# New orders for five instruction queues in a cross-attention and feed-forward kernel, with four accumulating transfers moved among them

## The chip, the core and the metric

The kernel runs on one core of a Trainium2 chip. The core has five engines with a queue of instructions each: PE (TensorE, matrix products), DVE (VectorE), ACT (ScalarE), POOL (GpSimd) and SP (SyncE, which here only issues transfers). Every queue runs strictly in the order in which the program wrote it; semaphores tie the queues together. Sixteen DMA engines carry the transfers. The metric is the device time of one execution in microseconds.

## What is computed

The input is x and a context of 4 batches, 512 rows, 256 columns, in float32. Two blocks follow each other.

```python
# attention by autocorrelation: the softmax weights of the best 6 delays
qf, kf = rfft(q, axis=1), rfft(k, axis=1)
corr = irfft(qf * conj(kf)).mean(axis=-1)          # one row of 512 delays per head
weights, delays = top_k(corr, 6)                   # softmax of the weights
out = sum(w * v rolled by each delay) @ Wo.T + bo
x = x + out
# feed-forward with 8-bit activations and weights of -1, 0, 1
def bitlinear(x, w, b):
    xq = act_quant(rmsnorm(x)); wq = weight_quant(w)
    return einsum('bsd,fd->bsf', xq, wq) + b
x = x + bitlinear(gelu(bitlinear(layernorm(x), w1, b1)), w2, b2)
```

## The kernel before

Fourier transforms are matrix products with constant matrices. The first 77 us transform, project and correlate the four batches; the change does not touch that part. From there on two things run beside each other.

The late attention of batch n (0 to 3): `inverse(n, c)` on PE brings the product back from the frequencies, ACT copies half of it (`inverse_copy`), DVE combines (`inverse_out`), PE projects (`project`), DVE adds to the residual and takes row sums (`add_residual`). Then ACT centres the rows (`centre`, L665) and squares them (`square_x`, L673), DVE takes the row maxima (`row_max`, L975) and scales (`x_scales`, L979, L983), ACT rounds to integers (`round_x`, L681), DVE casts them to bf16 (`whole_x`, L998) and SP issues a DMA transpose of them (L311). POOL computes the scale that the bias of the first layer needs, from values of DVE (`x_deq`, L988, L992; `x_rms`, L1296 to L1302; `aug_parts`, L1309 to L1315), and SP transposes that as well (L313, the `aug` rows). Both transposes of batch n must have landed before the first of its four tiles can enter the feed-forward.

The feed-forward runs in 16 tiles t of 128 rows, four per batch. One tile passes through: `up(t)` on PE (L492, L494, hidden layer of 1024), `gelu(t)` on ACT (L691), `hidden_max(t)` (L1041), `h_inverse(t)` (L1046), `quantise_h(t)` (L1053) and `whole_h(t)` (L1059) on DVE, `turn_h(t)` on PE (L506, a transpose), `copy_h(t)` on ACT (L706), `down(t)` on PE (L516), and `finish(t)` on DVE (L1067), which scales, adds to the residual `res` and releases the store on SP (L316). Aside, ACT squares the hidden rows (`square(t)`, L700) and POOL makes the scale of the result out of them (`h_rms(t)`, L1277, L1279; `h_deq(t)`, L1288, L1290).

The last bias b2 is added to `res` by a transfer that accumulates, 512 KB for each batch, issued by POOL:

```python
def add_b2(n):
    pool.wait_ge(s["xc_made"], n + 1)
    pool.dma_start(res[:, n], b2_all[:].unsqueeze(1).broadcast_to([P, NA, D]), accum_op=ALU.add).then_inc(s[f"b2_added{n}"], 16)
```

`finish(4n)`, the first of its batch, waits until it has landed. Buffers are double (psum banks of `up`, `hq`, `hq_t`, `xc`) or fourfold (`wf`, one hidden tile each), and each reuse waits for its last reader: `down(t)` waits for `finish(t-2)`, `up(t)` for `gelu(t-2)`, `gelu(t)` for `quantise_h(t-4)` and `square(t-4)`, `hidden_max(t)` for `h_deq(t-4)`.

Nothing schedules at run time: the order of each queue is a list of such calls, written out by hand in the kernel, one list for each of PE, ACT, DVE and POOL, and two loops for SP. These lists are what the change rewrites. The names in them are those above.

Of the kernel before, what the change touches and what calls it, by code (L numbers as in the profile page):

```python
# [98 lines left out]
def build(nc, x, ctx, wq_t, wkv_t, wo_t, bq, bkv, bo, w1_t, b1, w2_t, b2, c_forward, c_signal, c_eye, c_parts, out):  # L99
    es = ExitStack()  # L100
    with es:
# [175 lines left out]
        def _(sp):  # L277
# [31 lines left out]
            for n in range(NB):  # L309
                sp.wait_ge(s["xq_made"], n + 1)  # L310
                sp.dma_start_transpose(xq_t[:, n].rearrange("p a c r -> p (a c) r"), xq[:].rearrange("p a d -> p (a d)")).then_inc(s[f"xq_in{n}"], 16)  # L311
                sp.wait_ge(s["aug_made"], n + 1)
                sp.dma_start_transpose(aug_t[:, n], aug.rearrange("p a k -> p (a k)")).then_inc(s[f"aug_in{n}"], 16)  # L313
            for t in range(NA * NB):
                sp.wait_ge(s["y_made"], t + 1)
                sp.dma_start(out_v[:, t // NA, t % NA], res[:, t // NA, t % NA]).then_inc(s["stored"], 16)  # L316
            sp.wait_ge(s["stored"], 16 * NA * NB)

        LATE = 4 * 16
# [3 lines left out]
        def _(pe):  # L323
# [239 lines left out]
            turn_h(7)  # L563
            turn_h(8)
            down(6)
            up(11)
            turn_h(9)
            down(7)
            up(12)
            down(8)  # L570
            turn_h(10)
            up(13)
            down(9)
            turn_h(11)
            up(14)
            down(10)
            turn_h(12)
            up(15)
            down(11)
            turn_h(13)  # L580
            down(12)
            turn_h(14)
            down(13)
            turn_h(15)
            down(14)
            down(15)
# [3 lines left out]
        def _(act):  # L590
# [118 lines left out]
            inverse_copy(0, 1)  # L709
            copy_corr_even(1)  # L710
            exponents(1)
            act.activation(warm[:], half_neg[:, 0:1], ACT.Gelu)
# [5 lines left out]
            round_x(0)  # L718
            centre(1)
            inverse_copy(2, 0)  # L720
            gelu(0)
            square_x(1)
            gelu(1)
            inverse_copy(2, 1)
            gelu(2)
            square(0)
            round_x(1)
            gelu(3)
            square(1)
            square(2)  # L730
# [15 lines left out]
            gelu(7)  # L746
            copy_h(3)
            copy_h(4)
            square(6)
            square(7)  # L750
            gelu(8)
            square(8)
            copy_h(5)
            square_x(3)
            copy_h(6)
            gelu(9)
            round_x(3)
            square(9)
            gelu(10)
            copy_h(7)  # L760
            copy_h(8)
            square(10)
            gelu(11)
            copy_h(9)
            square(11)
            gelu(12)
            copy_h(10)
            square(12)
            gelu(13)
            copy_h(11)  # L770
            square(13)
            gelu(14)
            copy_h(12)
            square(14)
            gelu(15)
            copy_h(13)
            square(15)
            copy_h(14)
            copy_h(15)

# [2 lines left out]
        def _(dve):  # L783
# [315 lines left out]
            whole_x(1)  # L1099
            x_deq(1)  # L1100
            h_inverse(1)
            add_residual(2, 1)
            hidden_max(3)
            quantise_h(1)
            whole_h(1)
            inverse_out(3, 0)
            h_inverse(2)
            row_max(2)
            inverse_out(3, 1)
            x_scales(2)  # L1110
            quantise_h(2)
            hidden_max(4)
            whole_h(2)
            x_deq(2)
            h_inverse(3)
            add_residual(3, 0)
            h_inverse(4)
            hidden_max(5)
            add_residual(3, 1)
            h_inverse(5)  # L1120
            quantise_h(3)
            whole_x(2)
            quantise_h(4)
            whole_h(3)
            whole_h(4)
            quantise_h(5)
            finish(0)
            finish(1)
            row_max(3)
            finish(2)  # L1130
            whole_h(5)
            hidden_max(6)
            finish(3)
            h_inverse(6)
            hidden_max(7)
            quantise_h(6)
            h_inverse(7)
            finish(4)
            hidden_max(8)
            whole_h(6)  # L1140
            h_inverse(8)
            quantise_h(7)
            whole_h(7)
            x_scales(3)
            quantise_h(8)
            whole_h(8)
            x_deq(3)
            hidden_max(9)
            whole_x(3)
            finish(5)  # L1150
            h_inverse(9)
            quantise_h(9)
            whole_h(9)
            hidden_max(10)
            finish(6)
            h_inverse(10)
            quantise_h(10)
            whole_h(10)
            finish(7)
            hidden_max(11)  # L1160
            finish(8)
            h_inverse(11)
            quantise_h(11)
            whole_h(11)
            hidden_max(12)
            finish(9)
            h_inverse(12)
            quantise_h(12)
            whole_h(12)
            hidden_max(13)  # L1170
            finish(10)
            h_inverse(13)
            quantise_h(13)
            whole_h(13)
            hidden_max(14)
            finish(11)
            h_inverse(14)
            quantise_h(14)
            whole_h(14)
            hidden_max(15)  # L1180
            finish(12)
            h_inverse(15)
# [8 lines left out]
        def _(pool):  # L1191
# [139 lines left out]
            pool.wait_ge(s["out_half_made"], 2 * NC)  # L1331
            out_spectrum(3)
            x_rms(1)
            aug_parts(1)
            h_rms(0)
            h_deq(0)
            h_rms(1)
            add_b2(0)
            h_deq(1)
            x_rms(2)  # L1340
            aug_parts(2)
            h_rms(2)
            h_rms(3)
            h_rms(4)
            add_b2(1)
            add_b2(2)
            h_deq(2)
            h_deq(3)
            h_rms(5)
            h_deq(4)  # L1350
            h_rms(6)
            h_rms(7)
            h_deq(5)
            add_b2(3)
            h_deq(6)
            h_deq(7)
            x_rms(3)
            aug_parts(3)
            h_rms(8)
            h_deq(8)  # L1360
            h_rms(9)
            h_deq(9)
            h_rms(10)
            h_deq(10)
            h_rms(11)
            h_deq(11)
            h_rms(12)
            h_deq(12)
            h_rms(13)
            h_deq(13)  # L1370
# [41 lines left out]
```

## Time and profile before

| | us |
|---|---|
| median of 3 runs (lowest, highest) | 171.93 (171.16, 172.03) |
| the profiled execution | 171.91 |
| its span, first to last instruction | 170.1 |
| busy PE, DVE, ACT, POOL in the span | 151.2, 129.9, 98.7, 87.6 |

The profiled execution is 1.8 us longer than its span, and lies at the median. The busy times are sums over the whole span. What limits a stretch is read from the waits in it: which engine stands still, and what it waits for when it goes on. "issue" as the releaser of a wait means that the profile shows no instruction of an engine that ended then; often it is a transfer that landed. The start of the first instruction is 0 us in all views.

### The profile page before, as it was taken

The page shows a single profiled execution, that of the slowest core. Times are in us where ns is not written, and L with a number is a line of the kernel's source. Part 1 is how long each engine was busy: PE and PEld are TensorE (multiplying, and loading weights), DVE is VectorE, ACT ScalarE, POOL GpSimd, SP SyncE. Part 2 cuts the span into 40 slices and gives each one's busy share as a digit, 9 for nine tenths or more (in the row PEclk, how much of TensorE's full clock was granted, in tenths as well). Part 3 has the DMA queues.
Part 4 walks back from the last instruction along what each step waited for, and adds up shares of the span by engine and source line. Part 5 has one row for each costly group of instructions (what it writes and reads, how often), then busy time and mean ns, then how long its engine had stood idle before and what let it go on. Part 6 is the DMA issues. An engine that isn't in the chain of part 4 may idle for free.

```text
span 170.1 us, 2666 instructions
## 1 busy us (share of the span) xinstructions
PE 151.2 (89%) x808; PEld 103.9 (61%) x814; DVE 129.9 (76%) x325; ACT 98.7 (58%) x198; POOL 87.6 (51%) x156
## 2 busy tenths in 40 slices
PE   7889899999899999998999999799994499699853
PEld 2534689558654785756678854676763267457542
DVE  1546479999759996268578999999999139999982
ACT  3127624819570443120189189979998097999911
POOL 2040697945931000593943239678794706766330
PEclk9999999999999999999999999999999579999999
DMA  5989999162088000000000310046269760472012
GB/s 174 343 274 348 363 360 265 31 89 34 0 123 123 2 4 0 0 2 0 0 6 0 72 21 0 4 93 95 29 104 154 123 90 0 92 245 69 31 62 93
DMA packets 20529, 16.65 MB, mean 98 GB/s; under 512 B 7586, under 2 KB 19747, under 8 KB 20516
## 3 DMA queue, kind: packets, MB, share of 16 engines
q1 hardware_dynamic: 16292, 12.30, 24.1%
q0 software_dynamic: 4224, 4.19, 17.4%
q8 instruction: 6, 0.10, 0.2%
q14 instruction: 7, 0.06, 0.1%
HBM read 8.61 MB, written 2.10 MB: 63 GB/s over the span
## 4 chain that ended last, share of the span: by engine, by line
PE 45%; DVE 20%; ACT 11%; issue 11%; POOL 7%; DMA 4%; SPq 1%; DVEq 0%; POOLq 0%; ACTq 0%
PE psum L390 12%; PE psum L403 5%; DVE hmax L1041 4%; PE psum L474 4%; DMA res<-in_x 4%; PE psum L461 3%; PE psum L516 3%; DVE c_f L1053 3%; PE psum L332 3%; PE psum L333 3%; PE psum L492 2%; ACT kv_f L608 2%; PE psum L416 2%; ACT xn L673 2%; ACT xc_and_least L665 2%
## 5 line engine op out<-in xcount | busy, mean ns | idle before, releaser
L390 PE MATMUL psum<-wkv,c_f 128*128 128x512 f32 x64 | 29.0, 598 | 0.8 <-ACT c_f L595 0.8
L691 ACT ACTIVATE wf<-psum,xdeq 128x1024 f32<-128x1024 f32 x16 | 17.9, 1121 | 5.6 <-PE psum L494 5.6
L492 PE MATMUL psum<-w1q,xq_t 128*128 128x512 bf16 x58 | 15.8, 392 | 5.3 <-issue 5.2
L390 PEld LDWEIGHTS psum<-wkv,c_f 128*128 128x128 f32 x64 | 11.8, 190 | 13.7 <-issue 12.4
L614 ACT COPY kv_f<-psum 128x512 f32<-128x512 f32 x16 | 9.2, 582 | 18.1 <-PE psum L390 18.1
L1041 DVE TENSOR_REDUCE hmax<-wf 128x1 f32<-128x1025 f32 x16 | 19.3, 1212 | 0.1
L516 PE MATMUL psum<-w2q,kv_f 128*128 128x256 bf16 x128 | 17.1, 279 | 0.3 <-ACT kv_f L706 0.3
L461 PE MATMUL psum<-to_signal,out_f 128*128 128x256 f32 x64 | 15.1, 384 | 0.9 <-issue 0.8
L474 PE MATMUL psum<-wo,out_t 128*128 128x256 f32 x64 | 14.8, 385 | 1.2 <-DVE out_t L956 1.2
L403 PE MATMUL psum<-wq,x_f 128*128 128x256 f32 x64 | 15.1, 381 | 0.8 <-ACT x_f L595 0.8
L1220 POOL TENSOR_TENSOR kv_f<-kv_f,bkv_dc 1x512 f32<-1x512 f32 x4 | 5.7, 1417 | 19.0 <-ACT kv_f L614 19.0
L403 PEld LDWEIGHTS psum<-wq,x_f 128*128 128x128 f32 x64 | 12.0, 190 | 4.8 <-issue 3.5
L516 PEld LDWEIGHTS psum<-w2q,kv_f 128*128 128x128 bf16 x128 | 12.4, 101 | 3.6 <-ACT kv_f L706 0.4
L1067 DVE SCALAR_TENSOR_TENSOR res<-psum,hdeq,res 128x256 f32<-128x256 f32 x16 | 7.6, 476 | 8.4 <-issue 6.7
L474 PEld LDWEIGHTS psum<-wo,out_t 128*128 128x128 f32 x64 | 11.8, 190 | 3.5 <-DVE out_t L956 1.7
L461 PEld LDWEIGHTS psum<-to_signal,out_f 128*128 128x128 f32 x64 | 11.8, 190 | 3.4 <-issue 1.7
L506 PE MATMUL psum<-eye,kv_f 128*128 128x128 bf16 x128 | 9.9, 225 | 4.4 <-DVE kv_f L1059 3.1
L506 PEld LDWEIGHTS psum<-eye,kv_f 128*128 128x128 bf16 x128 | 8.4, 101 | 7.0 <-DVE kv_f L1059 5.6
L492 PEld LDWEIGHTS psum<-w1q,xq_t 128*128 128x128 bf16 x64 | 5.9, 99 | 10.9 <-issue 6.2
L1053 DVE TENSOR_SCALAR c_f<-wf,hinv 128x1024 int16<-128x1024 f32 x16 | 12.3, 766 | 0.3
L595 ACT COPY c_f<-psum 128x512 f32<-128x512 f32 x8 | 4.6, 586 | 12.9 <-PE psum L333 12.9
L706 ACT COPY kv_f<-psum 128x512 int32<-128x512 int32 x16 | 9.3, 594 | 4.4 <-PE psum L506 4.4
(167 smaller groups left out, 353.1 us busy)
## 6 DMA issues: line engine op xcount, KB each, us to landing
ctx_in<-in_ctx SPq DMA_DIRECT2D x4, 512.0 KB, 5.6
res<-in_x SPq DMA_DIRECT2D x4, 512.0 KB, 6.9
res<-bo_all POOLq DMA_DIRECT2D x4, 512.0 KB, 5.2
res<-b_all POOLq DMA_DIRECT2D x4, 512.0 KB, 7.1
out<-res SPq DMA_DIRECT2D x16, 128.0 KB, 1.8
wf<-in_w_t SPq DMA_DIRECT2D x1, 1024.0 KB, 9.5
wf<-in_w_t SPq DMA_DIRECT2D x2, 512.0 KB, 10.6
wkv<-in_wkv_t SPq DMA_DIRECT2D x1, 512.0 KB, 7.3
```

The lines of the kernel that those rows point to most:

```text
L390: mm = pe.matmul(bank(K_BANKS + ft), c_f[:, c, ft * P:(ft + 1) * P], wkv[:, c, :], start=(c == 0), stop=(c == NC - 1))
L403: mm = pe.matmul(psum[:, Q_BANKS + fam, part * D:(part + 1) * D], x_f[:, c, ft * P:(ft + 1) * P], wq[:, c, :], start=(c == 0), stop=(c == ...
L461: mm = pe.matmul(psum[:, I_BANKS + c, fam * D:(fam + 1) * D], out_f[:, n % 2, fam, part, c * P:(c + 1) * P], to_signal[:, ft, :], start=(f ...
L474: mm = pe.matmul(psum[:, O_BANKS + half, k * D:(k + 1) * D], out_t[:, c, SLOT[a], :], wo[:, c, :], start=(c == 0), stop=(c == NC - 1))
L492: pe.matmul(dst, xq_t[:, m, j, c, :], w1q[:, c, cols], start=(c == 0), stop=False)
L506: mm = pe.transpose(t_bank(t % 2)[:, k * P:(k + 1) * P], hq[:, t % 2, k * P:(k + 1) * P], eye16[:])
L516: mm = pe.matmul(psum[:, Y_BANKS + t % 2, 0:D], hq_t[:, t % 2, k, :], w2q[:, k, :], start=(k == 0), stop=(k == NK - 1))
L614: act.copy(kv_f[:, n, ft, :], bank(K_BANKS + ft)).then_inc(s["kv_copied"], 1)
L691: act.activation(hid[j], hb, ACT.Gelu, scale=xdeq[:, m, j:j + 1]).then_inc(s["hid_made"], 1)
L706: act.copy(hq_t[:, t % 2].rearrange("p k r -> p (k r)").bitcast(I32), t_bank(t % 2).bitcast(I32)).then_inc(s["ht_copied"], 1)
L1041: dve.tensor_reduce(hmax[:, j:j + 1], hid_and_least[j], AX.X, ALU.max, apply_absolute_value=True).then_inc(s["hmax_made"], 1)
L1053: dve.tensor_scalar(hround[:, t % 2, :], hid[j], hinv[:, j:j + 1], 127.0, ALU.mult, ALU.mult).then_inc(s["hround"], 1)
```

## The change

The lists of PE, ACT, DVE and POOL from the late attention on hold the same calls as before, each exactly once, in another order. SP's two loops become three functions and a written list. No instruction is added or removed, and none changes its size or its waits. The four calls of `add_b2` come later in POOL's list. The call that makes ACT load the table for Gelu moves from ahead of `centre(0)` to behind `round_x(0)`. The diff, cut to the parts that the prediction speaks of:

```diff
+            def bring_x(n):
                 sp.wait_ge(s["xq_made"], n + 1)
...
+            def store(t):
                 sp.wait_ge(s["y_made"], t + 1)
...
+            bring_x(2)
+            bring_aug(2)
+            store(0)
+            store(1)
+            store(2)
+            bring_x(3)
+            bring_aug(3)
+            store(3)
...
 PE
             up(4)
-            up(5)
             turn_h(0)
             project(3, 0)
             project(3, 1)
+            up(5)
             turn_h(1)
+            down(0)
             turn_h(2)
             up(6)
-            down(0)
             up(7)
             down(1)
-            down(2)
             turn_h(3)
             turn_h(4)
+            down(2)
             down(3)
             up(8)
             turn_h(5)
-            down(4)
             up(9)
             up(10)
             turn_h(6)
+            down(4)
             down(5)
...
 ACT
             square_x(2)
             gelu(4)
             square(3)
+            round_x(2)
+            copy_h(0)
             square(4)
             gelu(5)
-            copy_h(0)
-            round_x(2)
+            copy_h(1)
             centre(3)
-            copy_h(1)
             gelu(6)
+            square(5)
             copy_h(2)
-            square(5)
             gelu(7)
             copy_h(3)
+            square(6)
+            square_x(3)
             copy_h(4)
-            square(6)
+            gelu(8)
+            round_x(3)
+            gelu(9)
...
 DVE
             inverse_out(2, 0)
+            hidden_max(1)
             h_inverse(0)
+            inverse_out(2, 1)
+            h_inverse(1)
+            hidden_max(2)
             quantise_h(0)
-            whole_h(0)
-            inverse_out(2, 1)
-            hidden_max(1)
-            hidden_max(2)
             add_residual(2, 0)
             whole_x(1)
...
+            x_deq(3)
+            whole_h(7)
+            whole_x(3)
+            hidden_max(8)
             finish(4)
-            hidden_max(8)
-            whole_h(6)
             h_inverse(8)
...
+            finish(11)
-            h_inverse(14)
...
             quantise_h(15)
             whole_h(15)
+            finish(12)
             finish(13)
             finish(14)
             finish(15)
```

How the instructions now stand is seen best at two places. The first is POOL around the transfer of b2 for batches 1 and 2 (`res<-b_all`, where `x2` means two of them behind each other). Before it stood right behind the three `h_rms` of tiles 2 to 4, ahead of `h_deq(2)`:

```order
L1277 TENSOR_TENSOR hms<-hss,eps 128x1
L1279 TENSOR_TENSOR hr<-hms,half_neg 128x1
L1320 DMA res<-b_all 128x4x256 x2
L1288 TENSOR_TENSOR hm<-hmax,hr 128x1
L1290 TENSOR_TENSOR hdeq<-hm,wdeq 128x1
L1288 TENSOR_TENSOR hm<-hmax,hr 128x1
L1290 TENSOR_TENSOR hdeq<-hm,wdeq 128x1
L1277 TENSOR_TENSOR hms<-hss,eps 128x1
L1279 TENSOR_TENSOR hr<-hms,half_neg 128x1
```

Now the one for batch 1 stands alone behind `h_rms(5)`, ahead of `x_rms(3)` (lines have moved by 29 in the changed kernel):

```order
L1317 TENSOR_TENSOR hm<-hmax,hr 128x1
L1319 TENSOR_TENSOR hdeq<-hm,wdeq 128x1
L1317 TENSOR_TENSOR hm<-hmax,hr 128x1
L1319 TENSOR_TENSOR hdeq<-hm,wdeq 128x1
L1306 TENSOR_TENSOR hms<-hss,eps 128x1
L1308 TENSOR_TENSOR hr<-hms,half_neg 128x1
L1349 DMA res<-b_all 128x4x256
L1325 TENSOR_TENSOR xv<-xss,eps 128x4
L1327 TENSOR_TENSOR xve<-xv,eps 128x4
L1331 TENSOR_TENSOR xr<-xve,half_neg 128x4
```

The transfers of b2 thus moved behind later tiles: batch 1 behind `h_rms(5)`, batch 2 behind `h_deq(7)`, batch 3 behind `h_rms(12)`, where before they stood behind `h_rms(4)`, `h_rms(4)` and `h_deq(5)`.

The second place is ACT behind `square_x(2)`, where `xround` is the rounding of batch 2, `wf` a Gelu, `prod` and `x_f` the squares and `kv_f` a copy of a turned tile. Before:

```order
L673 ACTIVATE xn,xss<-xc_and_least 128x256 x4
L691 ACTIVATE wf<-psum,xdeq 128x1024
L700 ACTIVATE prod,hss<-wf 128x1024
L700 ACTIVATE x_f,hss<-wf 128x1024
L691 ACTIVATE wf<-psum,xdeq 128x1024
L706 COPY kv_f<-psum 128x512
L681 ACTIVATE xround<-xc_and_least,xscale 128x256 x4
L665 ACTIVATE xc_and_least<-res,row_sum 128x256 x4
```

And now:

```order
L702 ACTIVATE xn,xss<-xc_and_least 128x256 x4
L720 ACTIVATE wf<-psum,xdeq 128x1024
L729 ACTIVATE prod,hss<-wf 128x1024
L710 ACTIVATE xround<-xc_and_least,xscale 128x256 x4
L735 COPY kv_f<-psum 128x512
L729 ACTIVATE x_f,hss<-wf 128x1024
L720 ACTIVATE wf<-psum,xdeq 128x1024
L735 COPY kv_f<-psum 128x512
L694 ACTIVATE xc_and_least<-res,row_sum 128x256 x4
```

The rounding of batch 2 moved ahead of `square(4)`, `gelu(5)` and `copy_h(0)`.

## Rows read from the trace of the kernel before

**Rows 1.** The page's busy times and its clock row (40 slices of the span)

```profile
PE 151.2 (89%) x808; PEld 103.9 (61%) x814; DVE 129.9 (76%) x325; ACT 98.7 (58%) x198; POOL 87.6 (51%) x156
...
PEclk9999999999999999999999999999999579999999
```

**Rows 2.** Waits from 95 us on: us in total, times, longest

```profile
DVE res L1067 <- issue: 6.7, 2, 6.4
```

**Rows 3.** Timeline of DVE: start, duration, shape; in brackets the idle time before

```profile
105.15 1.38 DVE L1059 CAST kv_f<-c_f 128x1024 bf16<-128x1024 int16 x1
...
138.81 0.48 DVE L1067 SCALAR_TENSOR_TENSOR res<-psum,hdeq,res 128x256 f32<-128x256 f32 x1 [6.35 <-issue]
...
157.55 0.47 DVE L1067 SCALAR_TENSOR_TENSOR res<-psum,hdeq,res 128x256 f32<-128x256 f32 x1
...
160.39 0.47 DVE L1067 SCALAR_TENSOR_TENSOR res<-psum,hdeq,res 128x256 f32<-128x256 f32 x1
...
166.61 0.48 DVE L1067 SCALAR_TENSOR_TENSOR res<-psum,hdeq,res 128x256 f32<-128x256 f32 x1 [1.20 <-PE psum L516]
167.49 0.48 DVE L1067 SCALAR_TENSOR_TENSOR res<-psum,hdeq,res 128x256 f32<-128x256 f32 x1 [0.39 <-PE psum L516]
```

**Rows 4.** Timeline of PE around `up(8)` (the row at 134.04)

```profile
123.43 1.04 PE L516 MATMUL psum<-w2q,kv_f 128*128 128x256 bf16 x8
124.30 1.03 PE L492 MATMUL psum<-w1q,xq_t 128*128 128x512 bf16 x4
...
128.86 1.05 PE L516 MATMUL psum<-w2q,kv_f 128*128 128x256 bf16 x8 [0.26 <-ACT kv_f L706]
134.04 1.49 PE L492 MATMUL psum<-w1q,xq_t 128*128 128x512 bf16 x3 [4.12 <-issue]
```

**Rows 5.** Timeline of SP's two transposes of batch 2

```profile
123.67 1.23 SPq L311 DMA_TRANSPOSE xq_t<-xq  x1
124.95 2.58 SPq L313 DMA_TRANSPOSE aug_t<-c_sum  x1
```

**Rows 6.** Transfers issued between 108 and 121 us: KB, us to landing

```profile
res<-b_all POOLq DMA_DIRECT2D x1, 512.0 KB, 5.5
xq_t<-xq SPq DMA_TRANSPOSE x1, 3.0
aug_t<-c_sum SPq DMA_TRANSPOSE x1, 2.5
```

**Rows 7.** The same between 121 and 132 us

```profile
res<-b_all POOLq DMA_DIRECT2D x2, 512.0 KB, 9.2
xq_t<-xq SPq DMA_TRANSPOSE x1, 5.8
aug_t<-c_sum SPq DMA_TRANSPOSE x1, 8.6
```

**Rows 8.** POOL's line L1320 (`add_b2`), all four: its landings

```profile
DMA to landing us min/median/max: 5.5/7.1/10.4
```

**Rows 9.** Timeline of POOL: b2 for batches 1 and 2, and for batch 3

```profile
123.06 3.30 POOL L1320 DMA_DIRECT2D res<-b_all  x2
...
133.24 1.31 POOL L1320 DMA_DIRECT2D res<-b_all  x1
```

**Rows 10.** Timeline of ACT: table for Gelu, `centre(1)`, `square`, `gelu`, `copy_h`, `round_x`

```profile
86.00 1.28 ACT L712 ACT_TABLE_LOAD   x1
...
98.32 1.71 ACT L665 ACTIVATE xc_and_least<-res,row_sum 128x256 f32<-128x256 f32 x4 [4.24 <-DVE row_sum L966]
...
118.50 1.06 ACT L700 ACTIVATE x_f<-wf 128x1024 f32<-128x1024 f32 x1
...
119.54 1.11 ACT L691 ACTIVATE wf<-psum,xdeq 128x1024 f32<-128x1024 f32 x1
120.54 0.58 ACT L706 COPY kv_f<-psum 128x512 int32<-128x512 int32 x1
121.00 1.72 ACT L681 ACTIVATE xround<-xc_and_least,xscale 128x256 int16<-128x256 f32 x4
```

More of the change, by code:

```diff
@@ L711, in _ @@
             exponents(1)
-            act.activation(warm[:], half_neg[:, 0:1], ACT.Gelu)
             centre(0)
@@ L718, in _ @@
             round_x(0)
+            act.activation(warm[:], half_neg[:, 0:1], ACT.Gelu)
             centre(1)
@@ L721, in _ @@
             gelu(0)
+            gelu(1)
             square_x(1)
-            gelu(1)
             inverse_copy(2, 1)
             gelu(2)
+            round_x(1)
             square(0)
-            round_x(1)
             gelu(3)
@@ L736, in _ @@
             square(3)
+            round_x(2)
+            copy_h(0)
             square(4)
             gelu(5)
-            copy_h(0)
-            round_x(2)
+            copy_h(1)
             centre(3)
-            copy_h(1)
             gelu(6)
+            square(5)
             copy_h(2)
-            square(5)
             gelu(7)
             copy_h(3)
+            square(6)
+            square_x(3)
             copy_h(4)
-            square(6)
+            gelu(8)
+            round_x(3)
+            gelu(9)
+            copy_h(5)
+            gelu(10)
+            copy_h(6)
             square(7)
-            gelu(8)
             square(8)
[L753 to L757, printed above, removed]
+            copy_h(7)
             square(9)
-            gelu(10)
-            copy_h(7)
+            gelu(11)
+            square(10)
+            gelu(12)
             copy_h(8)
-            square(10)
-            gelu(11)
+            square(11)
+            gelu(13)
             copy_h(9)
-            square(11)
-            gelu(12)
+            square(12)
             copy_h(10)
-            square(12)
-            gelu(13)
-            copy_h(11)
             square(13)
             gelu(14)
+            gelu(15)
+            square(14)
+            copy_h(11)
+            square(15)
             copy_h(12)
-            square(14)
-            gelu(15)
             copy_h(13)
-            square(15)
             copy_h(14)
@@ L1091, in _ @@
             inverse_out(2, 0)
+            hidden_max(1)
             h_inverse(0)
+            inverse_out(2, 1)
+            h_inverse(1)
+            hidden_max(2)
             quantise_h(0)
-            whole_h(0)
-            inverse_out(2, 1)
-            hidden_max(1)
-            hidden_max(2)
             add_residual(2, 0)
             whole_x(1)
+            quantise_h(1)
             x_deq(1)
-            h_inverse(1)
+            hidden_max(3)
             add_residual(2, 1)
-            hidden_max(3)
@@ L1104, in _ @@
-            quantise_h(1)
+            whole_h(0)
+            h_inverse(2)
             whole_h(1)
+            quantise_h(2)
+            h_inverse(3)
             inverse_out(3, 0)
-            h_inverse(2)
+            inverse_out(3, 1)
             row_max(2)
-            inverse_out(3, 1)
+            quantise_h(3)
             x_scales(2)
-            quantise_h(2)
             hidden_max(4)
             whole_h(2)
-            x_deq(2)
-            h_inverse(3)
             add_residual(3, 0)
@@ L1117, in _ @@
             h_inverse(4)
+            add_residual(3, 1)
+            quantise_h(4)
+            x_deq(2)
+            whole_x(2)
+            whole_h(3)
             hidden_max(5)
-            add_residual(3, 1)
+            finish(0)
             h_inverse(5)
[L1121 to L1124, printed above, removed]
+            quantise_h(5)
             whole_h(4)
-            quantise_h(5)
-            finish(0)
+            hidden_max(6)
             finish(1)
@@ L1129, in _ @@
             row_max(3)
+            whole_h(5)
             finish(2)
-            whole_h(5)
-            hidden_max(6)
+            x_scales(3)
             finish(3)
             h_inverse(6)
+            quantise_h(6)
             hidden_max(7)
-            quantise_h(6)
+            whole_h(6)
             h_inverse(7)
+            quantise_h(7)
+            x_deq(3)
+            whole_h(7)
+            whole_x(3)
+            hidden_max(8)
             finish(4)
-            hidden_max(8)
@@ L1140, in _ @@
-            whole_h(6)
             h_inverse(8)
-            quantise_h(7)
-            whole_h(7)
-            x_scales(3)
             quantise_h(8)
-            whole_h(8)
-            x_deq(3)
             hidden_max(9)
-            whole_x(3)
             finish(5)
             h_inverse(9)
+            finish(6)
             quantise_h(9)
+            hidden_max(10)
+            whole_h(8)
             whole_h(9)
-            hidden_max(10)
-            finish(6)
+            finish(7)
             h_inverse(10)
+            hidden_max(11)
@@ L1157, in _ @@
             quantise_h(10)
[L1158 to L1161, printed above, removed]
+            hidden_max(12)
             h_inverse(11)
             quantise_h(11)
+            whole_h(10)
             whole_h(11)
-            hidden_max(12)
-            finish(9)
+            finish(8)
+            hidden_max(13)
             h_inverse(12)
             quantise_h(12)
+            h_inverse(13)
+            finish(9)
+            finish(10)
+            hidden_max(14)
@@ L1169, in _ @@
             whole_h(12)
-            hidden_max(13)
-            finish(10)
-            h_inverse(13)
             quantise_h(13)
+            h_inverse(14)
             whole_h(13)
-            hidden_max(14)
+            hidden_max(15)
+            quantise_h(14)
             finish(11)
-            h_inverse(14)
-            quantise_h(14)
+            h_inverse(15)
             whole_h(14)
-            hidden_max(15)
-            finish(12)
-            h_inverse(15)
             quantise_h(15)
@@ L1333, in _ @@
             x_rms(1)
+            h_rms(0)
             aug_parts(1)
-            h_rms(0)
+            h_rms(1)
             h_deq(0)
-            h_rms(1)
+            h_deq(1)
+            h_rms(2)
             add_b2(0)
-            h_deq(1)
             x_rms(2)
+            h_rms(3)
             aug_parts(2)
-            h_rms(2)
-            h_rms(3)
             h_rms(4)
-            add_b2(1)
-            add_b2(2)
             h_deq(2)
@@ L1363, in _ @@
             h_rms(10)
+            h_rms(11)
             h_deq(10)
-            h_rms(11)
+            h_rms(12)
+            add_b2(3)
             h_deq(11)
-            h_rms(12)
             h_deq(12)
```

46 lines of the change are left out of this document (31 added, 15 removed).

## The prediction

> **What bounds the kernel now.** I read the busy times first, then the waits of the late part, then the engines' timelines about the longest wait, and the transfers last. Over the whole span PE is busiest [rows 1], but the change begins behind 100 us, and there DVE sets the pace. Two numbers say so. A full round of DVE for one tile (`hidden_max`, `finish`, `h_inverse`, `quantise_h`, `whole_h`) takes 160.39 - 157.55 = 2.84 us, and DVE does such rounds back to back up to the tail [rows 3]; PE's share of a tile is `up` 1.30 us (six products of 512 columns, where eight of 256 take 124.30 - 123.43 = 0.87), `down` those 0.87, and `turn_h`, with half of `down`'s columns, 0.43, so 2.6 us [rows 4]. And from 102.39 us (`hidden_max(0)`) to 167.97 us (end of `finish(15)`) DVE stands still in four places only: 6.35 us ahead of `finish(4)`, 1.20 and 0.39 us ahead of the last two `finish` [rows 3], and 0.32 us more that make up the 6.7 us of two waits [rows 2].
>
> The 6.35 us have a history. `finish(4)` waits for `down(4)`, which stands behind `up(8)` on PE. `up(8)` stood ready from 129.9 us and began at 134.04, "issue" being its releaser [rows 4]: it waited for the transposes of batch 2. SP issued these at 123.67 and 124.95 us [rows 5]; they took 5.8 and 8.6 us to land [rows 7], the second so until 133.5 us, where those of batch 1 took 3.0 and 2.5 us [rows 6]. What lay beside them were two accumulating transfers of b2, issued from 123.06 us on [rows 9], with 9.2 us to landing as their median [rows 7] against 5.5 us for the one that went alone [rows 6]. While PE stood still its granted clock fell to 0.5, the level of 1.2 GHz [rows 1]: three matrix products of 0.5 us pitch instead of 0.22 [rows 4]. So `up(8)`, `turn_h(5)` and `down(4)`, 2.6 us of work, took from 134.04 until `finish(4)` could begin at 138.81.
>
> **The change, on paper.** No work is added or removed, so the new end follows from where engines will stand still. I laid out the four lists from 102.39 us on, each call at the later of its engine being free and its waits being met, with pitches (start to start) from rows: ACT `gelu` 1.00, `copy_h` 0.47, `square` 1.04, `centre`, `square_x` and `round_x` 1.6 each [rows 10]; PE as above; DVE 1.13 for a maximum, 0.78 for `quantise_h`, 0.34 for a cast, 0.39 for `finish` and 0.12 for `h_inverse`, together 2.8 [rows 3] (only the sum has a row here); POOL 1.3 for issuing b2 [rows 9] and, rounded, 0.8 for `h_rms` and 0.6 for `h_deq`, on which nothing below rests closely. The steps that decide:
>
> 1. *Start.* `whole_h(0)` took 1.38 us [rows 3] where a cast takes 0.4, and stood ahead of `inverse_out(2, 1)`. Now it stands behind. `inverse_out(2, 1)` ends at 106.1 instead of 107.2, PE projects 1.1 us earlier, `whole_x(1)` ends at 109.1, the aug rows of batch 1 are ready at 111.5, and with 2.5 us to land `up(4)` begins at 114.2 instead of 114.9.
> 2. *Transposes of batch 2.* ACT has `square_x(2)` done at 115.6, `gelu(4)`, `square(3)` at 117.7 and `round_x(2)` at 119.3. DVE reaches `x_deq(2)` and `whole_x(2)` at 121.1 to 121.8 (1.8 us earlier), POOL makes the aug rows until 122.6. SP issues at 121.8 and 123.1, and alone they land at 124.9 and 125.6.
> 3. *b2 of batch 1* now waits behind `h_rms(5)`, so for `square(5)`, done at 126.05: issue at 126.9, behind these transposes. That is the separation.
> 4. *`up(8)`* is then held by PE itself: `down(2)` and `down(3)`, the latter behind `copy_h(3)` at 128.0, end at 128.9. It begins at 128.9, 5.1 us earlier, and PE never stands still long enough to repeat the 4.1 us ahead of the clock's fall; the longest gap I find is 1.1 us.
> 5. *Batch 3 of x* is brought forward: `square_x(3)` until 130.6, `round_x(3)` until 133.7, `whole_x(3)` at 133.8 to 134.15, transposes at 134.2 and 135.5, landed by 138.1. `up(12)` wants them at 140.1 only. DVE waits 0.3 us for `round_x(3)`. SP has only three stores ahead, released by 128.5; `store(3)` and later ones queue for 7 us, and nobody waits for them but the end.
> 6. *`finish(4)`* begins at 135.3 instead of 138.81, with `hidden_max(8)`, `whole_h(6)`, `quantise_h(7)`, `whole_h(7)` and batch 3's scales, cast and x_deq (3.7 us of DVE work) already behind it.
> 7. *From there to the end* DVE has 22.5 us of work by the pitches (12 `finish`, 8 `h_inverse`, `quantise_h` and casts each, 7 maxima), and waits 0.4 us ahead of `hidden_max(14)` and 1.35 us in the tail, where `turn_h(15)`, `copy_h(15)` and `down(15)` follow `whole_h(15)` as before. ACT has 21.5 us left from 133.7 and PE 20 us from 134.8, both less than DVE. `finish(15)` ends near 159.9, before any stretching.
>
> The same as a sum over DVE: idle before 8.26 us and the stretched cast 1.04 make 9.3. New idle: 0.3 ahead of `whole_x(3)`, 0.4 ahead of `hidden_max(14)`, 0.4 in hand-overs, 1.35 in the tail, 2.45 in all. Gain 6.85 us. The 1.6 us by which DVE's other rows in this stretch exceeded their pitches I let recur. Span 170.1 - 6.85 = 163.25; with the 1.8 us outside it, 165.1 us. The profiled execution was at the median, so nothing is corrected.
>
> **Edits at nothing.** The table load of 1.28 us moves into a stretch in which ACT stood idle for 4.24 us [rows 10], and it held nobody where it was. If that cover were gone it would cost 1.3 us. The last store begins at the end of `finish(15)` as before.
>
> **Where the new waits can bite: b2.** The transfers had slack before and have little now. `finish(4)` at 135.3 needs a landing after issue at 126.9: 8.4 us of room. `finish(8)` at 146.4 needs one after issue at 139.2 (behind `square(7)`, `h_rms(7)` and `h_deq(7)`): 7.2 us. `finish(12)` at 156.8, issue 148.4: 8.4 us. What stands behind each on DVE is everything, and `down(6)`, `down(10)`, `down(14)` wait for them. Landings ran 5.5 to 10.4 us [rows 8]; alone 5.5, beside another b2 and transposes 8.0 and more. In the new order none has a transpose or a second b2 beside it, so I take 5.5 to 7, at no cost; at 10.4 each the three would cost 2.0, 3.2 and 2.0 us if they did not absorb each other, about 5 together since a late one delays the next deadline more than the next issue. Stores of 128 KB do lie beside the second and third.
>
> A row bears on POOL's side as well: two issues took 3.30 us, one 1.31 [rows 9], and the cast of 1.38 us lay beside a POOL operation [rows 3]. The Trainium skill, page "SBUF — State Buffer", section "🔬 SBUF: two separate sides", says that DVE in a two-port mode (casts and `tensor_scalar` among them) locks GpSimd out while it writes the descriptors of its own transfers, so that such a transfer starves. By that rule this change puts b2 of batches 2 and 3 into DVE's densest stretch and the landings go to the long end; the trace, where a stretched issue cost 0.3 us, bears it out weakly.
>
> **Rivals.**
> - *b2 lands late.* The landings take about 10 us because POOL's issue is stretched or stores share the DMA engines; DVE waits ahead of `finish(4)`, `(8)` and `(12)`. For it: 10.4 was seen. Against it: only with a second transfer and two transposes beside. Time 165.1 + 5 = 170 us. Chance 0.15.
> - *The transposes were slow by themselves.* If 5.8 and 8.6 us were not b2's doing but SP's (its second issue took 2.58 us [rows 5]), they land at 131.7, `up(8)` is 2.8 us late and `up(12)` 4.0 us, of which the first delay covers most: 165.1 + 4 = 169 us. Against it: batch 1 with 3.0 and 2.5 [rows 6]. Chance 0.06.
> - *Slower than before.* The place is `finish(8)`, whose queue is in order. If b2 of batch 2 lands L us after its issue, all behind it moves by L - 7.2. Slower begins at L = 7.2 + 6.8 = 14.0 us; with 15.5 the time is 173.4 us. It takes five stores and a starved issue together; the largest L seen is 10.4. Chance 0.05.
> - *The wait only moves.* ACT has no slack from 115.7 to 139 us in my layout; if each of its steps comes 5% late with PE behind, the 6.35 us come back as many small waits of DVE, and the time stays near 171.5. Against it: in the tail of before the same calls ran beside DVE's rounds of 2.84 us without a wait [rows 3]. Chance 0.04.
>
> **The numbers.** The forecast has 0.70, with its own range of 163.2 (no stretches recur) to 167.5 (b2 a little late, some hand-overs more). The whole range goes to 169.5, into the first two rivals, and down to 162.8. A measurement of this kernel tells about 0.5%, 0.9 us, from no change. Faster: 0.70, 0.13 of the first rival's 0.15, 0.06 of the second and a little of the last, 0.90. Same: 0.05. Slower: 0.05.
>
> **What will show it.** Right: no wait of DVE ahead of a `finish` above 1.5 us; `up(8)` begins near 129 with PE's clock at full level throughout; every transpose lands within 3.5 us and each b2 within 7.5; `finish(4)` near 135. Wrong: "issue" ahead of `finish(4)`, `(8)` or `(12)` (b2), ahead of `up(8)` or `up(12)` (transposes), or DVE's idle time spread over many small waits for ACT.

## The result and the profile after

The changed kernel takes 165.32 us (median of 4 runs, 164.24 to 165.50) against 171.55 us for the one before (median of 4, 170.93 to 172.03): a ratio of 0.963, with a 95% interval of 0.957 to 0.968. The forecast was 165.1 us. The profiled execution took 165.38 us with a span of 163.6. An execution more than 1.5% above the fastest of its kernel counts as slow and stays out of the ratios below: there is one of the kernel before (174.0 us) and one in experiment 8 (169.06 us).

The first rows to read are those that answer to [rows 1]. Every engine is busy for as long as before, within 2 us (the largest difference is DVE's, 129.9 against 128.2), in a span that is 6.5 us shorter, and PE's clock never fell:

```profile
PE 150.5 (92%) x814; PEld 102.9 (63%) x814; DVE 128.2 (78%) x325; ACT 98.9 (60%) x198; POOL 87.3 (53%) x156
...
PEclk9999999999999999999999999999999999999999
```

DVE's waits from 100 us on, in the changed kernel (us in total, times, longest), answer to [rows 2]. The wait of 6.4 us on "issue" is gone, and no wait on a transfer is left; nine short ones that are left sum to 3.8 us:

```profile
DVE res L1096 <- PE psum L545: 2.0, 4, 1.3
...
DVE hmax L1070 <- ACT wf L720: 0.7, 2, 0.5
DVE res L995 <- PE psum L503: 0.6, 2, 0.4
...
DVE kv_f L1088 <- PE psum L535: 0.5, 1, 0.5
```

The timeline of PE about `up(8)` (start, duration) answers to [rows 4]. `up(8)` is the row at 129.94, right behind `down(2)` and `down(3)`, and has no idle time before it:

```profile
127.66 0.61 PE L535 MATMUL psum<-eye,kv_f 128*128 128x128 bf16 x8 [0.21 <-ACT kv_f L735]
128.10 2.01 PE L545 MATMUL psum<-w2q,kv_f 128*128 128x256 bf16 x16
129.94 1.03 PE L521 MATMUL psum<-w1q,xq_t 128*128 128x512 bf16 x4
```

The transfers answer to [rows 5 to 9]. First SP's and POOL's timelines in the changed kernel: the second transpose of batch 2 is issued 3.9 us ahead of b2 of batch 1, and those of batch 3 lie between two transfers of b2:

```profile
122.75 1.23 SPq L312 DMA_TRANSPOSE xq_t<-xq  x1
124.02 1.27 SPq L316 DMA_TRANSPOSE aug_t<-c_sum  x1
...
135.19 1.23 SPq L312 DMA_TRANSPOSE xq_t<-xq  x1
```

```profile
127.88 1.44 POOL L1349 DMA_DIRECT2D res<-b_all  x1
...
140.53 1.34 POOL L1349 DMA_DIRECT2D res<-b_all  x1
```

And what was issued between 119.5 and 132 us, with the us to landing:

```profile
res<-b_all POOLq DMA_DIRECT2D x1, 512.0 KB, 7.1
...
xq_t<-xq SPq DMA_TRANSPOSE x1, 3.2
aug_t<-c_sum SPq DMA_TRANSPOSE x1, 2.5
```

The landings of all four b2, which answer to [rows 8]:

```profile
DMA to landing us min/median/max: 5.5/5.9/7.1
```

Last, three `finish` of DVE in the changed kernel, tiles 4, 14 and 15, which answer to [rows 3]. `finish(4)` comes without a wait at 136.21, and the tail has its 1.26 and 0.39 us as before:

```profile
136.21 0.47 DVE L1096 SCALAR_TENSOR_TENSOR res<-psum,hdeq,res 128x256 f32<-128x256 f32 x1
...
160.09 0.48 DVE L1096 SCALAR_TENSOR_TENSOR res<-psum,hdeq,res 128x256 f32<-128x256 f32 x1 [1.26 <-PE psum L545]
160.96 0.48 DVE L1096 SCALAR_TENSOR_TENSOR res<-psum,hdeq,res 128x256 f32<-128x256 f32 x1 [0.39 <-PE psum L545]
```

One offset has to be taken out before two traces are laid over each other. The part that the change does not touch ended at different times: the first transpose is issued at 94.94 us in the trace of before and at 95.81 in that of after, and over the thirteen traces of this study it lies near 94.6 to 95.0 or near 95.7 to 96.1, in both groups with old and with new orders. The offset is there long before the change begins: PE's third group of Fourier products starts at 24.27 us in the trace of before and at 25.15 in that of after. Below, "late part" is the span less the start of that first transpose: 75.2 us before, 67.8 us after, 7.4 us less. The times that were measured differ by 6.2 us. So a median of a few executions can be off by about 1 us for this reason alone, and steps below 1 us are read from the late part. That is one trace for each kernel, and before has a second spread: its executions have a mean granted clock of PE of 0.98, with spans from 169.9 us, or of 0.99, with spans from 169.0, and the profiled one is of the first kind. Its 75.2 us, and with it the first step of the ladder below, may be too large by up to about 1 us.

### The profile page after: what moved, and what is told of

Read it like the earlier page. It is cut to its first block and busy times, and to the rows that moved or that the text cites. A ratio compares the mean times of both kernels' runs of the same rounds, so it can differ in the third digit from the quotient of the medians.

```text
span 163.6 us, 2672 instructions
## 1 busy us (share of the span) xinstructions
PE 150.5 (92%) x814; PEld 102.9 (63%) x814; DVE 128.2 (78%) x325; ACT 98.9 (60%) x198; POOL 87.3 (53%) x156
## 5 line engine op out<-in xcount | busy, mean ns | idle before, releaser
L545 PE MATMUL psum<-w2q,kv_f 128*128 128x256 bf16 x128 | 16.2, 273 | 1.4 <-ACT kv_f L735 1.4
L521 PE MATMUL psum<-w1q,xq_t 128*128 128x512 bf16 x64 | 16.4, 379 | 0.9 <-issue 0.9
L490 PE MATMUL psum<-to_signal,out_f 128*128 128x256 f32 x64 | 15.1, 384 | 0.9 <-issue 0.8
L432 PE MATMUL psum<-wq,x_f 128*128 128x256 f32 x64 | 15.1, 381 | 0.8 <-ACT x_f L624 0.8
L1249 POOL TENSOR_TENSOR kv_f<-kv_f,bkv_dc 1x512 f32<-1x512 f32 x4 | 5.2, 1294 | 19.6 <-ACT kv_f L643 19.6
L545 PEld LDWEIGHTS psum<-w2q,kv_f 128*128 128x128 bf16 x128 | 11.7, 98 | 5.0 <-ACT kv_f L735 3.4
L535 PE MATMUL psum<-eye,kv_f 128*128 128x128 bf16 x128 | 9.4, 219 | 1.9 <-ACT kv_f L735 1.1
L1308 POOL TENSOR_TENSOR hr<-hms,half_neg 128x1 f32<-128x1 f32 x16 | 10.4, 648 | 1.3
```

The lines of the kernel that those rows point to most:

```text
L432: mm = pe.matmul(psum[:, Q_BANKS + fam, part * D:(part + 1) * D], x_f[:, c, ft * P:(ft + 1) * P], wq[:, c, :], start=(c == 0), stop=(c == ...
L490: mm = pe.matmul(psum[:, I_BANKS + c, fam * D:(fam + 1) * D], out_f[:, n % 2, fam, part, c * P:(c + 1) * P], to_signal[:, ft, :], start=(f ...
L521: pe.matmul(dst, xq_t[:, m, j, c, :], w1q[:, c, cols], start=(c == 0), stop=False)
L535: mm = pe.transpose(t_bank(t % 2)[:, k * P:(k + 1) * P], hq[:, t % 2, k * P:(k + 1) * P], eye16[:])
L545: mm = pe.matmul(psum[:, Y_BANKS + t % 2, 0:D], hq_t[:, t % 2, k, :], w2q[:, k, :], start=(k == 0), stop=(k == NK - 1))
L1308: pool.tensor_tensor(hr[:, p], hms[:, p], half_neg[:, 0:1], ALU.pow).then_inc(s["hr_made"], 1)
```

## The experiments

**1. b2 apart, nothing else.** The kernel before, with POOL's list changed in three places:

```diff
-            add_b2(1)
-            add_b2(2)
...
             h_rms(5)
+            add_b2(1)
...
-            add_b2(3)
...
             h_deq(7)
+            add_b2(2)
...
             h_rms(12)
+            add_b2(3)
```

> The kernel before with one edit: add_b2(1), (2), (3) stand on POOL behind h_rms(5), h_deq(7) and h_rms(12), as in the changed kernel; all other lists as before. Theory (b2 beside the transposes made the wait): the transposes of batch 2 land in 3.0 and 2.5 us, up(8) begins at 129.9 instead of 134.0 us, finish(4) at about 133.9 (held by b2 of batch 1, issued at 128.3), DVE's wait of 6.35 us shrinks to 1.4, PE's clock stays at full level; time 171.5 - 5 = 166.6 us, about 0.97 of before. Rival (the order of the other queues brings most of it): time 169 us or more.

Measured: 168.15 us, ratio 0.976 (0.969 to 0.984). The transfers issued between 119.5 and 132 us, with the us to landing, and after them DVE's waits for b2:

```profile
res<-b_all POOLq DMA_DIRECT2D x1, 512.0 KB, 6.6
xq_t<-xq SPq DMA_TRANSPOSE x1, 3.3
aug_t<-c_sum SPq DMA_TRANSPOSE x1, 2.6
```

```profile
DVE res L1067 <- DMA res<-b_all: 2.1, 1, 2.1
```

The transposes are fast again and the clock stays up, as the theory said; the late part is 71.0 us, 4.2 less than before. The gain was to be 5, and the time 166.6 us: b2 of batch 1 landed after 6.6 us, not 5.5, and DVE waited 2.1 us for it instead of 1.4, and the untouched part came out 0.85 us longer than in the trace of before. So separating alone brings more than half, and it makes a smaller wait of its own.

**2. The collision put back into the changed kernel.** On POOL:

```diff
             h_rms(3)
+            add_b2(1)
+            add_b2(2)
             aug_parts(2)
             h_rms(4)
             h_deq(2)
             h_deq(3)
             h_rms(5)
-            add_b2(1)
...
-            add_b2(2)
```

> The changed kernel with one edit: add_b2(1) and (2) stand together behind h_rms(3), so that they are in flight when the transposes of batch 2 are issued. Theory: issued at 119.6 to 121.2 us, they overlap the transposes issued near 122.8 and 124.0; these land after 4 to 6 and 6 to 9 us, up(8) begins 1.5 to 3 us late; time 167 to 168.5 us. Rival (only the orders of the other queues count, or the transposes are slow by themselves): 165.3 us.

Measured: 166.52 us, ratio to before 0.967 (0.962 to 0.973), late part 69.0 us, 1.2 more than the changed kernel. That is a little less than expected. From issue to landing the two transposes took 15.1 us in sum, against 14.4 in [rows 7], and PE waited for them (transfers issued between 119.5 and 132 us; then PE's row of `up(8)`):

```profile
res<-b_all POOLq DMA_DIRECT2D x2, 512.0 KB, 7.7
...
xq_t<-xq SPq DMA_TRANSPOSE x1, 8.2
aug_t<-c_sum SPq DMA_TRANSPOSE x1, 6.9
```

```profile
131.64 1.02 PE L521 MATMUL psum<-w1q,xq_t 128*128 128x512 bf16 x4 [1.65 <-DMA xq_t<-xq]
```

But b2 had been issued 3.0 us ahead of the first transpose (119.62 against 122.62; in before it was 0.6 us), so all had landed by 131.5 us. PE's wait was 1.65 us, and the clock did not fall. A wait of that length is no safeguard, though: in experiment 5 PE waits 1.63 us at the same call, and there the clock falls. The mechanism holds in both kernels; its price depends on how long after PE's readiness the last transpose lands (1.5 us here, 3.6 in before) and on whether the clock falls.

**3. No b2 at all in the kernel before** (b2 is left out of the output): `add_b2` issues nothing, `finish` does not wait.

> The kernel before without the four transfers of b2 and the waits for them (the bias b2 is left out of the output). Theory: the wait of 6.35 us ahead of finish(4) goes nearly whole, time 171.5 - 6 = 165.5 us, less than with b2 apart by what its landing still costs there (1.4 us). Rival (the transposes are slow by themselves): transposes of 5.8 and 8.6 us remain and the time stays near 171.

Measured: 166.17 us, ratio 0.968 (0.962 to 0.974), late part 69.7 us. The transposes of batch 2 took 3.2 and 2.5 us, so they are not slow by themselves. DVE's wait ahead of `finish(4)` is down to nothing, 0.9 us of new waiting appears for `x_rms(3)`, and the gain is 5.5 us of late part, not 6.

**4. No b2 in the changed kernel** (b2 is left out of the output).

> The changed kernel without the four transfers of b2 and the waits for them (the bias b2 is left out of the output). Theory (in the new order b2 costs nothing): 165.3 us, at most 0.4 less. Rival (b2 still holds finish or slows transfers): 164 us or less.

Measured: 164.78 us, ratio 0.958 (0.952 to 0.963), late part 67.75 us against 67.8. The time is 0.5 us less than that of the changed kernel, where the forecast allowed 0.4, but the single executions pair off (165.31, 165.15, 164.41 and 164.22 against 165.50, 165.38, 165.27 and 164.24), so no cost is to be seen. In the new order the four transfers cost nothing: 2 MB of accumulating traffic that cost the old order 5.5 us is hidden.

**5. Plain copies instead of accumulating ones.** In the kernel before, for batches 1 and 2 (b2 is left out of their output):

```diff
-                pool.dma_start(res[:, n], b2_all[:]..., accum_op=ALU.add)
+                pool.dma_start(kv_f[:, n]..., b2_all[:]...)
```

> The kernel before, where the transfers of b2 for batches 1 and 2 are plain copies of the same 512 KB each into a free tile instead of accumulating ones (b2 is left out of the output for those batches). Theory A (any traffic of POOL beside a transpose slows it): the transposes land after 5 to 6 and 8 to 9 us, the time is 171.5. Theory B (accumulating is what costs, since a DMA engine reads its target as well): the transposes land in 3 to 4 us each, time about 166.5.

Measured: 170.25 us, ratio 0.988 (0.981 to 0.995), late part 72.4 us, between the two theories. The transfers issued between 119.5 and 132 us, and PE's row of `up(8)`:

```profile
kv_f<-b_all POOLq DMA_DIRECT2D x2, 512.0 KB, 5.1
xq_t<-xq SPq DMA_TRANSPOSE x1, 6.4
aug_t<-c_sum SPq DMA_TRANSPOSE x1, 6.4
```

```profile
132.68 1.61 PE L492 MATMUL psum<-w1q,xq_t 128*128 128x512 bf16 x4 [1.63 <-issue]
```

Plain traffic delays a transpose too: 6.4 us against 3.2 and 2.5 alone. The accumulating pair took longer to land (9.2 us as its median against 5.1), and beside it the second transpose took 8.6 us; that this transpose is late because the pair lasts longer fits, but was not tested apart. DVE's wait ahead of `finish(4)` fell from 6.35 to 3.62 us. PE stood still for only 1.63 us, yet its clock fell as `up(8)` began: the four products took 1.61 us where they take 1.03 at full clock. So part of what is left against experiment 3 (72.4 against 69.7 us) is the clock.

**6. The start on DVE.** The kernel of experiment 1 and

```diff
-            whole_h(0)
             inverse_out(2, 1)
+            whole_h(0)
```

> The kernel before with b2 apart (as in the first experiment) and inverse_out(2, 1) ahead of whole_h(0) on DVE. Theory: whole_h(0) no longer takes 1.4 us where PE waits for inverse_out(2, 1), up(4) begins 0.7 us sooner, and the time is 0.5 to 0.8 us less than with b2 apart alone. Rival: later queues absorb it, no difference from b2 apart.

Measured: 166.36 us, ratio 0.968 (0.964 to 0.972), late part 70.1 us, 0.9 less than experiment 1, a little above the 0.5 to 0.8 of the theory. The medians differ by 1.8 us, but the untouched parts of the two traces differ by 1.2 (first transpose at 94.60 against 95.79 us).

**7. `finish(4)` later.** The kernel of experiment 6 and

```diff
-            finish(4)
             hidden_max(8)
             whole_h(6)
             h_inverse(8)
             quantise_h(7)
+            finish(4)
```

> The kernel of the experiment on the start (before, b2 apart, inverse_out(2, 1) ahead of whole_h(0)) with one more edit on DVE: finish(4) stands behind hidden_max(8), whole_h(6), h_inverse(8) and quantise_h(7). Theory (what is left against the changed kernel, 2.3 us, is the 2.0 us for which DVE stood still ahead of finish(4) until b2 of batch 1 had landed): 2.4 us of DVE work now lie over that wait, and the time falls by 1.5 to 2.0 us to 164.3 to 164.9. Rival (the earlier x steps of batch 3 and the other moves of PE and ACT bring it): at most 0.8 us less, 165.6 or more.

Measured: 165.27 us, ratio 0.9615 (0.957 to 0.966), late part 68.6 us, 1.5 less than experiment 6, and the wait for b2 is gone from DVE's waits. The work now lies over it. The median fell by 1.1 us only and misses the forecast of 164.3 to 164.9 by 0.4; four of the six executions took 165.02 to 165.47 and two 166.09 and 166.37. It is still below the rival's 165.6. With this the old lists, with five calls moved, are within 0.8 us of late part of the full rewrite.

**8. b2 of batch 2 later in the changed kernel**, behind `h_deq(9)`:

```diff
             h_deq(7)
-            add_b2(2)
...
             h_deq(9)
+            add_b2(2)
```

> The changed kernel with add_b2(2) two tiles later on POOL, behind h_deq(9) instead of h_deq(7). Theory (room of 7.1 us between issue and finish(8), of which a landing takes 5.5 to 7): issue near 143.3 us instead of 140.5, finish(8) 1.1 to 2.7 us late, time 166.4 to 168. Rival (the room is larger, or the loss is absorbed): 165.3.

Measured: 166.55 us (median of three executions, 165.82 to 167.25), ratio 0.969 (0.963 to 0.975), late part 70.8 us, 3.0 more than the changed kernel. POOL's issue and DVE's `finish(8)`:

```profile
143.36 1.34 POOL L1349 DMA_DIRECT2D res<-b_all  x1
```

```profile
148.87 0.48 DVE L1096 SCALAR_TENSOR_TENSOR res<-psum,hdeq,res 128x256 f32<-128x256 f32 x1 [2.37 <-DMA res<-b_all]
```

Counted from the first transpose it was issued 4.0 us later than in the changed kernel (143.36 - 94.61 against 140.53 - 95.81), and DVE waits 2.37 us, so 1.6 us had been in hand, as the room of 7.1 us less a landing of 5.5 says. The mechanism of the rival on the slow side is real, and its point is where the prediction put it. Not all of the 3.0 us is that wait: counted from the first transpose, `finish(8)` is 2.45 us late, and then PE's clock falls in the tail of this trace too (length, PE, PEld, DVE, ACT, POOL, then granted clock, DMA share, GB/s):

```profile
156.00:158.00 2.00, 2.00 (x11) 1.36 (x10) 1.36 (x5) 0.60 (x2) 1.12 (x2) 0.50 0.01 2
```

**9. SP's stores last in the changed kernel**, as the old loops had them:

```diff
-            store(0)
-            store(1)
-            store(2)
             bring_x(3)
             bring_aug(3)
+            store(0)
+            store(1)
+            store(2)
```

> The changed kernel with SP's list as before: store(0) to (2) behind the transposes of batch 3 instead of ahead. Theory: nobody waits for stores but the end, so 165.3 us within 0.4. Rival (stores beside the transposes of batch 3 or b2 of batch 2 slow them): b2 of batch 2 or the transposes land later by 1 us and more, 166 us.

Measured: 164.31 us, ratio 0.959 (0.952 to 0.965): no cost. The time is 1.0 us below the forecast of 165.3, as is the next experiment's: executions of the changed kernel itself lie near 164.2 or near 165.4. Three executions took 164.26 to 164.32 us; the profiled one took 166.12, and its trace shows where the time went: PE's clock fell in the tail, and its late part is 69.3 us, 1.5 more than that of the changed kernel. The 24 products of 256 columns that begin at 154.18 us took 4.45 us, where the same ones of the changed kernel took 2.91. Busy time of each engine in three stretches of it (length, PE, PEld, DVE, ACT, POOL, then granted clock, DMA share, GB/s):

```profile
150.00:152.00 2.00, 1.38 (x13) 0.72 (x11) 1.54 (x3) 1.62 (x3) 1.64 (x7) 1.00 0.74 144
152.00:154.00 2.00, 0.88 (x13) 0.74 (x14) 2.00 (x5) 2.00 (x5) 1.47 (x4) 1.00 1.19 198
154.00:156.00 2.00, 2.00 (x17) 1.50 (x14) 1.08 (x2) 1.12 (x3) 1.56 (x5) 0.57 0.33 57
```

And the same place of the changed kernel's own trace, 0.8 us later, with the same order on PE:

```profile
151.00:153.00 2.00, 1.16 (x12) 0.64 (x10) 1.59 (x3) 1.62 (x3) 1.56 (x7) 1.00 0.88 166
153.00:155.00 2.00, 1.10 (x17) 0.96 (x18) 2.00 (x4) 2.00 (x4) 1.38 (x5) 1.00 1.19 200
155.00:157.00 2.00, 2.00 (x21) 1.59 (x19) 1.85 (x6) 1.49 (x4) 1.80 (x4) 1.00 0.19 34
```

**10. The Gelu table back ahead of `centre(0)`** in the changed kernel.

> The changed kernel with the Gelu table loaded ahead of centre(0), as before. Theory: the load of 1.28 us lies in ACT's idle time in both places, 165.3 us within 0.3. Rival: the time at centre(0) matters, 0.4 us or more either way.

Measured: 164.28 us, ratio 0.959 (0.955 to 0.963), late part 67.8 us, the same to 0.1 us. The time is 1.0 us under the forecast of 165.3, which by itself would be the rival's sign; but the offset is there at 24.10 us against 25.15, long before the table is loaded at 85.73 us. And the first transpose, at 94.66 us, starts where it does in two traces with the table in its new place (94.61 and 94.71 in experiments 8 and 11). So no effect is seen.

**11. A better tail for the changed kernel**, on PE and on ACT:

```diff
             turn_h(12)
-            turn_h(13)
             down(11)
+            turn_h(13)
             down(12)
-            down(13)
             turn_h(14)
+            down(13)
             turn_h(15)
...
             gelu(15)
-            square(14)
             copy_h(11)
-            square(15)
+            square(14)
             copy_h(12)
+            square(15)
```

> The changed kernel with another tail: PE has down(11) ahead of turn_h(13) and turn_h(14) ahead of down(13), ACT has copy_h(11) and copy_h(12) one square earlier. Theory (PE and ACT, not DVE, lose 1.3 us behind whole_h(15) because turn_h(14) queues behind three downs): finish(15) starts 0.5 to 0.8 us earlier, time 164.6 to 164.8 us. Rival (the end is set by DVE's work up to whole_h(15)): 165.3 us.

Measured: 163.67 us (163.61 to 163.85, 6 runs), ratio 0.954 (0.951 to 0.958), so faster than before beyond doubt. Its interval overlaps slightly with that of the changed kernel (0.957 to 0.968). Experiment 10, timed beside it and as fast as the changed kernel by its late part, is the closer comparison: 164.28 us (164.11 to 165.37, 6 runs), above every run here. The late part is 67.3 us, 0.5 less than that of the changed kernel, as the theory said. The forecast of the time, 164.6 to 164.8, started from 165.3, and this trace is of the group whose untouched part is 1 us shorter. DVE's wait ahead of `finish(14)` fell from 1.26 to 0.84 us:

```profile
158.51 0.48 DVE L1096 SCALAR_TENSOR_TENSOR res<-psum,hdeq,res 128x256 f32<-128x256 f32 x1 [0.84 <-PE psum L545]
```

The late parts of the traces make a ladder, from one edit to the next (one trace each; the steps hold in this order of edits):

| | late part, us | step |
|---|---|---|
| before | 75.2 | |
| b2 apart | 71.0 | -4.2 |
| and `whole_h(0)` behind `inverse_out(2, 1)` | 70.1 | -0.9 |
| and `finish(4)` behind four calls of tiles 6 to 8 | 68.6 | -1.5 |
| all the new orders | 67.8 | -0.8 |
| and the better tail | 67.3 | -0.5 |

## Why the prediction was right

The number was right and so was nearly every step under it. Laid beside the trace of after, less the 0.88 us by which its `hidden_max(0)` came later (103.27 against 102.39):

| step of the prediction | forecast | trace less 0.88 |
|---|---|---|
| 1: `up(4)` begins | 114.2 | 114.2 |
| 2: transposes of batch 2 issued | 121.8, 123.1 | 121.9, 123.1 |
| 3: b2 of batch 1 issued | 126.9 | 127.0 |
| 4: `up(8)` begins | 128.9 | 129.1 |
| 5: `whole_x(3)` begins | 133.8 | 133.9 |
| 6: `finish(4)` begins | 135.3 | 135.3 |
| b2 of batch 2 issued; `finish(8)` | 139.2; 146.4 | 139.7; 146.7 |
| 7: `finish(15)` ends | 159.9 | 160.6 |

*What bounds the kernel.* Right. Where DVE stands still the time is lost, and what made it stand still longest was a transpose held by b2: experiments 1 and 3 take b2 away from the transposes in the old order, experiment 2 puts it back in the new one, and the landings go with it each time.

*The sum.* Several terms offset each other. 1.6 us of stretched DVE rows were booked to recur. From `hidden_max(0)` to the end of `finish(15)` DVE's busy time fell from 55.76 to 53.51 us, by 2.25, where the sum counted 1.04 for the one stretched cast: 1.2 of the 1.6 us did not recur. Its idle time in the same stretch, with the gaps too short to be listed as waits, fell from 9.82 to 4.66 us, by 5.16, where the sum had 8.26 less 2.45, or 5.81. So the stretch became 7.41 us shorter instead of 6.85. Against that, the part ahead of the change, which the sum took as fixed, came out 0.9 us longer in the profiled execution. The agreement within 0.2 us is partly luck. The prediction also took a single trace as the origin; traces differ by about 1 us there.

*b2 in its new places.* Booked at no cost with 5.5 to 7 us to land: they took 5.5 to 7.1, and experiment 4 finds no cost. But the margin was small, as stated, and experiment 8 shows it: 4.0 us later on POOL costs 2.37 us of wait.

*The rule on descriptors.* The Trainium skill, page "SBUF — State Buffer", section "🔬 SBUF: two separate sides", has it that GpSimd's own transfers starve while DVE works in a two-port mode. For b2 of batches 2 and 3 the issues took 1.34 and 1.29 us, as long as that of batch 0 (1.33), and the landings 5.5 and 6.2 us. B2 of batch 1 took 1.44 and 7.1 us, with stores beside it; without those (experiment 9) it took 1.45 and 6.4. The trace does not bear the rule out as a cost, but it is a weak test: casts of DVE lay beside the issue of batch 2 for 0.65 us and a `quantise_h` beside that of batch 3 for 0.4 us.

*The rivals.* "b2 lands late": no. "The transposes were slow by themselves": no, experiment 3. "The wait only moves": no, DVE's waits are short and few. "Slower than before" needed a landing above 14 us; the largest seen in any run here is 10.4.

*What was not seen ahead.* The same collision has two prices. Experiments 1 and 2 put it at 4.2 us in one order and at 1.2 in the other, for transposes that take about as long to land; in the second, b2 also started earlier ahead of them and the clock stayed up, and the share of each was not measured apart. And step 4 read the clock wrongly: it took 4.1 us of idle time as what lies ahead of a fall. In the trace of before the granted clock is 1.00 up to 131.5 us and 0.52 from there to 132, so it fell 1.6 us after PE stopped at 129.9. It fell after 1.63 us of idle time in experiment 5, and in the tails of experiments 8 and 9, in the latter with no gap above 0.88 us just before. The changed kernel's own four executions kept a mean granted clock of at least 0.999, so the conclusion held there, but not by the reason given.

## What to carry to other kernels

Look at which transfers are in flight when a transfer that someone waits for is issued, and issue the ones with slack at another time; where they are waited for can stay as it is. Here three calls on POOL were worth 4.2 us. A transfer that was moved has a new deadline; put DVE work, or that of whatever engine waits, over its landing before it becomes the next wait (1.5 us here). When two traces are compared, subtract what the untouched part did, and look at the granted clock of both.

## What the runs showed of the hardware

- A DMA transpose of 256 KB landed in 3.0 to 3.4 us and one of 128 KB in 2.4 to 2.7 us with no transfer of POOL beside them. Beside two plain copies of 512 KB they took 6.4 and 6.4 us, beside two accumulating ones 5.8 and 8.6 (before), and 8.2 and 6.9 when those had a start of 3 us (experiment 2).
- SP's own issue of a transpose got longer beside that traffic: 1.2 to 1.3 us alone, 2.58 for the second one in before, 1.94 and 2.63 in experiment 2, 3.27 for the second one in experiment 5.
- Accumulating transfers landed later than plain copies of the same size: a pair took 9.2 us as its median where plain copies in the same place, into another tile, took 5.1.
- PE's granted clock fell to the level of 1.2 GHz in four of the thirteen traces. In before it fell 1.6 us into a wait of 4.12 us. In experiment 5 it fell just after a wait of 1.63 us, while a wait of 1.65 us at the same call in experiment 2 left it up. In the tail of experiment 9 it fell where the longest idle time of PE just before was 0.88 us, after 4 us in which it was busy for 1.38 and 0.88 of 2.00 us each; in the changed kernel, with 1.16 and 1.10 us, it did not fall. It also fell in the tail of experiment 8. So the length of one idle gap did not decide it. The execution of experiment 9 with the fall took 1.8 us longer than its siblings; by the late part, 1.5 us of that came with the fall.
